# A second attention with its first turns written out, and twelve of the last sixteen roundings on the Pool engine

## What is computed

```python
h = _layernorm(x, axis=-1)
# L1_xattn: 16 heads of 8, queries from h, keys and values from ctx
scores = jnp.einsum('bthd,bshd->bhts', wq, wk) / jnp.sqrt(jnp.float32(DH))
probs = jax.nn.softmax(scores, axis=-1)
attn = jnp.einsum('bhts,bshd->bthd', probs, wv)
x = x + jnp.tanh(g_xattn[1]) * (attn.reshape(b, t, d) @ wo_w.T + wo_b)
# L1_ffn: layernorm, then two linear layers on rounded numbers
xq = jnp.clip(jnp.round(x * scale), -128.0, 127.0)   # act_quant, scale = 127 / largest of the row
h = jax.nn.gelu(qlinear(layernorm(x), w1, b1))
x = x + jnp.tanh(g_ffn[1]) * qlinear(h, w2, b2)      # act_quant again, on the 512 hidden numbers
```

## Time and profile before

| | us |
|---|---|
| median of 3 runs | 400.61 |
| lowest and highest run | 398.65, 400.82 |
| the profiled execution: its time | 397.01 |
| the profiled execution: its span | 394.9 |
| busy in the span: PE, DVE, ACT, POOL | 367.7, 321.5, 262.1, 219.5 |

### The profile page before, as it was taken

How to read it: one execution, slowest core, us unless ns; L and a number is a source line. 1 busy time by engine, 2 the same in 40 slices (tenths; PEclk the granted TensorE clock), 3 DMA queues, 4 the chain that set the end, 5 groups by cost and what they waited for, 6 DMA issues and landing times. The chain is left out here.

```text
span 394.9 us, 10468 instructions
## 1 busy us (share of the span) xinstructions
PE 367.7 (93%) x3588; PEld 272.4 (69%) x3601; DVE 321.5 (81%) x916; ACT 262.1 (66%) x528; POOL 219.5 (56%) x380
## 2 busy tenths in 40 slices
PE   7799989999999999999999999999979999986785
PEld 6356656666676676667766788878867888765664
DVE  2989999899998998988746588756458899999796
ACT  2377767777777777776765222245658999887885
POOL 4655559666666667762604000007685887788653
PEclk9899999999999999999999999999999999999589
DMA  5989999900000000000000000000000000000003
GB/s 166 259 151 123 121 135 118 108 1 2 2 2 2 2 1 2 2 2 2 3 1 2 0 2 0 2 1 2 0 2 2 3 4 2 2 4 2 0 16 93
DMA packets 61034, 13.26 MB, mean 34 GB/s; under 512 B 51108, under 2 KB 60344, under 8 KB 60984
## 3 DMA queue, kind: packets, MB, share of 16 engines
q1 hardware_dynamic: 60196, 12.37, 22.9%
q10 hardware_dynamic: 660, 0.23, 0.2%
q0 software_dynamic: 128, 0.00, 0.0%
HBM read 11.55 MB, written 1.05 MB: 32 GB/s over the span
## 5 line engine op out<-in xcount | busy, mean ns | idle before, releaser
L407 POOL TENSOR_TENSOR a_rn<-a_ssq,neghalf 128x8 f32<-128x8 f32 x48 | 79.0, 1653 | 24.4 <-DVE a_ssq L1019 19.8
L90 POOL TENSOR_TENSOR nrow<-mrow 128x2 f32<-128x2 f32 x32 | 6.3, 196 | 56.8 <-DVE mrow L86 56.5
L1019 DVE TENSOR_REDUCE a_ssq<-q_home 128x8 f32<-128x512 f32 x48 | 32.2, 672 | 6.4 <-ACT q_home L798 6.2
L501 PE MATMUL a_x<-wkv_a,a_kvT 128*128 128x512 f32 x64 | 35.5, 637 | 1.2 <-ACT a_kvT L791 1.0
L804 ACT ACTIVATE kv_home<-a_x,maskcol 128x512 f32<-128x512 f32 x32 | 21.9, 684 | 19.9 <-PE a_x L501 19.9
L423 POOL TENSOR_TENSOR a_yr<-a_ymv,eps_row 128x1 f32<-128x1 f32 x16 | 3.0, 189 | 37.8 <-DVE a_ymv L1062 37.8
L1038 DVE TENSOR_REDUCE a_mx<-a_s 128x4 f32<-128x512 f32 x32 | 21.9, 686 | 2.0 <-PE a_s L527 1.9
L1950 DVE TENSOR_REDUCE b_mx<-b_s 128x16 f32<-128x1024 f32 x16 | 19.5, 1218 | 4.3 <-PE b_s L1548 4.0
L515 PEld LDWEIGHTS a_m<-ident,q_home 128*128 128x128 f32 x128 | 15.8, 143 | 9.7 <-issue 9.0
L816 ACT ACTIVATE kv_home<-a_m,cols 128x512 f32<-128x512 f32 x32 | 21.9, 685 | 0.6 <-PE a_m L515 0.4
L546 PE MATMUL a_m<-kv_home,p_home 128*64 128x65 f32 x512 | 22.0, 228 | 0.3 <-ACT p_home L826 0.3
(11 more groups left out here) (301 smaller groups left out, 1144.6 us busy)
## 6 DMA issues: line engine op xcount, KB each, us to landing
w_gu<-in_L_ffn_Wg_dram SPq DMA_DIRECT2D x4, 512.0 KB, 9.7
w_gu<-in_L_ffn_Wu_dram SPq DMA_DIRECT2D x4, 512.0 KB, 11.9
w_d<-in_L_ffn_Wd_dram SPq DMA_DIRECT2D x8, 256.0 KB, 8.0
out_dram<-xs SPq DMA_DIRECT2D x8, 128.0 KB, 1.8
xs<-in_x_dram SPq DMA_DIRECT2D x1, 640.0 KB, 7.6
cs<-in_ctx_dram SPq DMA_DIRECT2D x1, 640.0 KB, 9.1
wkv_a<-in_L_xattn_Wkv_dram SPq DMA_DIRECT2D x2, 256.0 KB, 6.6
nat<-in_L_ffn_w_dram SPq DMA_DIRECT2D x2, 256.0 KB, 3.2
```

The costliest lines, as they stand in the source:

```text
L407: nc.gpsimd.tensor_tensor(rn[:, tp, i, :], ssq[:, tp, i, :], neghalf[:, 0:H0], ALU.pow)\
L501: nc.tensor.matmul(p_x[:], kvT[:, tp, b * 2 * S:(b + 1) * 2 * S], wkv_a[:, INNER:2 * INNER], start=True, stop=True).then_inc(vproj_done, 1)
L1019: nc.vector.tensor_reduce(ssq[:, tp, i, :], sq[:, i, :].rearrange("p (h d) -> p h d", h=H0), AX.X, ALU.add).then_inc(reduced, 1)
```

## The change

`project(1)`, `turn_context(4)` and `turn_input(4)` leave the combination, with ScalarE's steps for them, and come behind `scores(0)`. The turns 1 to 3 of TensorE's loop and 0 to 2 of ScalarE's are written out in a new order. Pool makes the normalised inputs 5 and 6 inside the combination and spreads the keys of tile 2 before anything else. `busy` is four matmuls in place of six, and earlier. Two waits on the bank `p_k` are set to suit (L1516, L1572). In the tail `ROUNDED_BY` gives 12 tiles to Pool (7 before), 4 to ACT (6 before), none to DVE (3 before), and the lists of all engines from turn 16 on are put in another order. Nothing else is added or dropped: DVE has three instructions less and Pool five more, ACT two less.

```diff
-        ROUNDED_BY = "PAPAPADPAPPDPAAD"
+        ROUNDED_BY = "PPPPPAAPPPPPPAAP"
...
-                if t in (0, 1, 3, 5, 7):
+                if t in (0, 1, 3, 5, 7, 9, 12):
                     pool.wait_ge(rooted, (t + 1) // 2 + 1)
                     normalise((t + 1) // 2)
...
             spread_keys(1)
+            spread_keys(2)
             for s in range(NT):
-                if s >= 3:
+                if s >= 4:
                     spread_keys(s - 1)
-                if exists(s + 5, NT):
+                if s >= 2 and exists(s + 5, NT):
                     normalise(s + 5)
...
-                wait(pe, att_ready, t - 6)
+                wait(pe, att_ready, t - 6 if t > 6 else t - 5)
...
-                    pe.wait_ge(xT_ready, min(t + 7, NT))
+                    pe.wait_ge(xT_ready, min(t + 7, NT) if t else 6)
...
             pe.wait_ge(zeroed, 3)
+            scores(0)
+            project(1)
+            turn_context(4)
+            turn_input(4)
+            busy(nc, p_m[:, 0:P], ident[:], ident[:], 4)
+            scores(1)
+            project(2)
             pe.wait_ge(tern_out, 2)
-            for s in range(1, NT):
+            probs_T(0, 0)
+            probs_T(0, 1)
+            turn_context(5)
+            turn_input(5)
+            project(3)
+            mix(0, 1)
+            mix(0, 0)
+            scores(2)
+            project(4)
+            turn_context(6)
+            probs_T(1, 0)
+            probs_T(1, 1)
+            turn_attention(0, 0)
+            turn_input(6)
+            turn_context(7)
+            turn_input(7)
+            for s in range(4, NT):
...
-            turn_norm(10, 0)
             out_proj(12, 0)
+            turn_norm(10, 0)
...
+            turn_hidden(2)
             turn_norm(14, 0)
+            up(13, 1)
             down(1)
-            turn_hidden(2)
+            turn_norm(15, 1)
             up(14, 0)
-            turn_norm(15, 1)
```

More of the change, by code:

```diff
@@ L1843, in _ @@
                 if t == 13:
[L1844 removed]
                     input_out(3)
[L1846 to L1854 removed]
+            keys_out(1)
+            context_out(4)
+            queries_out(1)
+            values_out(1)
+            input_out(4)
+            exp(0, 0)
+            keys_out(2)
+            queries_out(2)
+            probs_out(0, 0)
+            probs_out(0, 1)
+            values_out(2)
+            context_out(5)
+            input_out(5)
+            exp(1, 1)
+            keys_out(3)
+            queries_out(3)
+            values_out(3)
+            context_out(6)
+            keys_out(4)
+            queries_out(4)
+            probs_out(1, 0)
+            probs_out(1, 1)
+            values_out(4)
+            attention_out(0, 0)
+            exp(2, 0)
+            input_out(6)
+            context_out(7)
+            input_out(7)
+            queries_out(5)
+            keys_out(5)
+            for s in range(3, NT):
                 if exists(s + 2, NT):
```

155 lines of the change are left out of this document (66 added, 89 removed).

## The result

| | before | after |
|---|---|---|
| median of 20 runs each, us | 399.35 | 403.36 |
| lowest and highest run | 396.79, 402.07 | 400.14, 409.65 |
| the profiled execution: time, span | 397.01, 394.9 | 400.14, 398.3 |

The ratio of after to before is 1.0083, with a 95% interval of 1.0053 to 1.0114; it leaves out after's five slow runs (407.64 to 409.65 us, granted clock 0.950 to 0.957), which the medians and the highest run above still hold. The change makes the kernel slower, by 0.8%.

What follows compares the result with a forecast made beforehand. TensorE and DVE were taken as full in the middle, so the opening's end decides. Profiled 397.0 + 3.1 (opening) - 0.8 (tail) = 399.3; the difference of 2.3 added to the median gave 402.9 us, 8-in-10 range 398.2 to 405.6.

Steps and rivals of the forecast that it cites:

- Combination: Stretch ahead of the attention: shorter by two turns and a projection, so `scores(0)` starts at 285.8, 2.3 us earlier.
- Point 1: Opening, from `scores(0)` to `scores(1)`: `scores(1)` starts at 289.4, 4.1 us earlier.
- Point 2: Opening, up to `scores(2)`: `exp(1)` waits behind input(5)'s copy until 294.1 to 294.2; `scores(2)` at 295.7, lead down to 1.6 us.
- Point 3: Opening, up to `exp(2)`: `project(4)` and `turn_attention(0)` wait for values; `exp(2)` at 300.6, a lead of 0.6 us.
- Point 4: Opening, up to `scores(3)`: inputs 6 and 7 and context(7) stand behind `exp(2)`; `scores(3)` at 305.2, a lag of 3.1 us.
- upper bound of 3.6: Opening: largest lag in us at `scores(3)`, if each of some ten hand-offs is dearer by 0.05.
- No way to make it good in the middle: Middle of the attention: TensorE and DVE are full, so any lead or lag at `scores(3)` reaches the tail unchanged.
- The first rival: Opening: TensorE's clock falls to half rate for 3.4 us, costing 1.7 us, to 404.6 us; chance 0.18.
- The tail: End of the kernel: moved roundings and new order make it 0.8 us shorter; bounds 2.9 shorter to 0.4 longer.
- The −0.3 at the end: Tail: with the third rounding on Pool, the last turn can start at 388.9, not 389.20, 0.3 us sooner.
- Tail order: Ahead of `scores(15)`: `turn_norm(10)` behind `out_proj(12)` makes the second mix wait for its copy, costing 0.3 us.
- Pool against DVE: Tail: busy Pool delays five `hidden_bound` scalings on DVE by 0.61 each, +3.0 us, to 405.9 us; chance 0.07.

Runs made afterwards that it cites:

- e9_line_early: Changed kernel with inputs 6 and 7 turned and copied ahead of `turn_attention(0)` and `exp(2)`, plus idle matmuls; 400.27 us, ratio 1.0037 to the kernel before.
- the other opening: Changed kernel with `scores(1)` placed where input(5) allows, no input held back, and the old loop entered at turn 3; 394.70 us, ratio 0.9930 to before.
- opening only: Changed kernel with the lists from turn 16 on and `ROUNDED_BY` put back as before; 403.66 us, ratio 1.0156 to before.

## Why the prediction was right, and where it was not

The time came out at 403.36 where 402.9 was said, slower by 0.8% where slower had the highest chance. The mechanism, the line of inputs held back behind values and exponents, is what the traces show, and e9_line_early shows that a part of the lag goes with it. That the two times lie within half a microsecond is in part luck, as the sum at the end of this section shows. By its steps:

- **Combination.** `scores(0)` 2.16 us sooner; said 2.3. Right.
- **Point 1.** `scores(1)` 3.86 sooner; said 4.1. Right.
- **Point 2.** `exp(1)` is held behind the copy of input(5), as said (293.10, in times of before 294.43 against 294.1 to 294.2). `scores(2)` is 0.99 sooner; said 1.6. The mixes of tile 0 started at 293.89 + 1.33 = 295.22, 0.6 later than the sum had them (294.6). Half of it stands ahead of the turn of input(5), at 293.93 where the sum comes to 293.64: `scores(1)` was 0.2 late, and the way from `project(2)` to ScalarE was dearer by 0.1. The other half is one mis-sized term, a turn and the projection behind it: from the start of the turn of input(5) to the mixes it took 1.29 us, and the sum has 0.96 (0.07 and 0.89). `project(3)` did not wait for input(5): it needs input(3), and multiplied that at 293.13, before the copy of input(5) ended at 293.21.
- **Point 3.** `turn_attention(0)` waits for the values of tile 4, as said. `exp(2)` is 0.07 later than before where it was to be 0.6 sooner: the 0.6 us of point 2, carried on. (Against point 3, `project(4)` started with the end of `scores(2)`, at 295.55, and not behind the values of tile 3, out at 295.12.)
- **Point 4.** Context(7) and input(7) come behind `exp(2)`, as said. From the turn of input(7) to `scores(3)` the sum had 2.4 us; the two kernels with both holes filled and this order on TensorE took 2.67 at full clock (303.49 to 306.16 in the first). It is the same term again: from that turn to the end of the projection 1.31 us, where the sum had 1.0. So the lag of order is 3.9 us, not 3.1, and outside its own upper bound of 3.6: that bound was made for dearer hand-offs, while of the gap of 0.8, 0.5 is what the turn of input(7) was late by (303.34 in times of before, said 302.8) and 0.3 the longer way from there to `scores(3)`.
- **No way to make it good in the middle.** 6.59 at `scores(4)`, 6.69 at `scores(15)`. Right, and the other opening shows that it holds for a lead as well.
- **The clock.** The first rival came true, the fall of the clock in the opening, on top of the forecast and not in its place: TensorE's clock fell in or behind the holes in after and in the three kernels that kept this opening without both holes filled. It cost 2.7 us where 1.7 was priced, since it was down for 6.8 us and not 3.4. That rival should have had more than 0.18. What spoke against it, that 2.18 us of work in 4 had kept the clock at 1.00, was true of one hole in one execution; here were two, with one turn at a time in the second. The Trainium skill (TensorE: Matmul & The Clock Gate, Part 1) has activity release the throttle and an idle stretch bring it back; the trace agrees here, with 0.85 us of work in 4 and then 1.2 GHz. By the rule the fall was sure, and on that the page was nearer than the chance I gave.
- **The tail.** From `scores(15)` 1.95 shorter. The 0.8 that was said has 0.3 of order ahead of `scores(15)` in it, so for this stretch 1.1 was said. At 6.8 us of half clock in both, the lists of before take 32.66 (opening only) and those of after 31.56: 1.1 us is the change's, and 0.85 is half clock that the tail of after did not have. Within the 1.1, the three roundings are about 0.8 by their own experiment. The −0.3 at the end did not come: from the last factor to the last turn it is 1.30 us (391.31 to 392.61), 1.31 before. The last turn doesn't wait for the rounding that is gone; it stands behind matmuls of `down(6)` at 392.17, and these wait for DVE's `final`, which starts at 391.41. It was so before as well, and the sum had missed it: there `down(6)` starts at 388.76, 0.44 ahead of the turn, as here.
- **Tail order.** The +0.3 for `turn_norm(10)` behind `out_proj(12)` is there, at 0.17. It lies ahead of `scores(15)`, and so not in the column end − s(15). From `scores(14)` to `scores(15)` before takes 4.35 us and after 4.52:

```profile
354.77 0.69 PE L1548 MATMUL b_s<-b_k,b_q 32*64 32x256 f32 x16 [0.25 <-issue]
...
359.12 0.69 PE L1548 MATMUL b_s<-b_k,b_q 32*64 32x256 f32 x16 [0.25 <-issue]
```

```profile
359.96 0.69 PE L1554 MATMUL b_s<-b_k,b_q 32*64 32x256 f32 x16
...
364.48 0.69 PE L1554 MATMUL b_s<-b_k,b_q 32*64 32x256 f32 x16
```

  All eight kernels with the new tail have 4.51 to 4.56 there, all three with the old one 4.34 to 4.35. So the lag at `scores(15)` holds 0.17 of the tail's order, and the tail's own gain, taken from `scores(14)`, is 1.78 us.
- **Pool against DVE.** `hidden_bound` took 311 ns a piece, 238 before, 0.6 us in all for eight, and not 3.0. With ten roundings on Pool it was 163. The rival falls here. The Trainium skill (SBUF — State Buffer, on the two separate sides) has DVE and GpSimd lock a port pair; the trace agrees: four of the eight were long, 0.41 to 0.51 us, and each of these ended within 0.03 us of the end of a pass of Pool that had begun before it, while the other four took 0.15 to 0.18. But it does not set the time: the tail came out shorter.

The sum for the profiled execution was 399.3 with before's early part. After's has 400.14 with an early part 1.33 shorter, so 401.5 on the same footing: 2.2 above. Of this 0.8 is order and 2.7 clock in the opening; the tail with its order gave 1.78 in place of 0.8, which takes off 0.1 by the change itself and 0.85 by its clock: 2.5. The rest to 2.2 is that after has 0.3 us less around its span (1.84, before 2.11). The median of before that the forecast stood on (400.61, three runs) was 1.3 above the one of twenty, and this hid most of the miss: from before to after the medians moved 4.0, and 2.3 was said. By the ratio it is 3.3 us.

## To carry to other kernels

Follow the step that shares a bank or a buffer with others (here context, input, context, input through `p_k`) as a line of its own, and put none of its copies behind a long instruction or a wait that it does not need: an early score is worth nothing if the inputs that the next turns need come later for it. A lead or a lag at the entry of a stretch in which two engines are full went through whole here (0.72 and 6.6 us), so an opening is judged by when its last turn ends and not by its first. When a hole is opened on TensorE, price the work behind it at half clock as well, and part order from clock with idle matmuls before judging an order.
